# Four chained layers on one core: blocks for the mixed matrices made by ScalarE and GpSimd from rows loaded twice, and the mask multiplied on the returning mixed matrix

## The reference, cut to what matters

```python
x = x + L0(x, cond_8)   # top 2 of 8 experts per batch + one shared expert: (gelu(x Wg) * (x Wu)) Wd, inner width 1024
x = x + L1(x, cond_8)   # w_bot = einsum('bg,got->bot', y, weight * mask[None]); x @ w_bot^T + bias
x = x + L2(x, cond_8)   # x W_base^T + b_base + 2 * lora, ranks weighted by cond_8
x = x + L3(x, cond_8)   # one of 8 experts per batch: (silu(x Wu + bu) * (x Wg + bg)) Wd + bd, inner width 512
```

## Time and profile before

| | us |
|---|---|
| median of three runs | 1377.16 |
| lowest and highest | 1370.75, 1379.93 |
| the profiled execution | 1381.71 |
| its span, first to last instruction | 1380.1 |
| PE busy | 1278.1 (93%) |
| DVE busy | 707.0 (51%) |
| POOL busy | 619.6 (45%) |
| ACT busy | 414.5 (30%) |
| share of span that DMA queues' packets took | 16.6% SyncE's, 14.7% GpSimd's |

### The profile page before, as it was taken

The page is one execution under the profiler, slowest core; times in us unless marked ns, Lnnn a source line. Parts: engine busy times, 40 slices in busy tenths (PEclk is TensorE's granted clock), DMA queues, the critical chain, the costliest instruction groups (busy, mean ns, idle before and its releaser), DMA issues.

```text
span 1380.1 us, 29485 instructions
## 1 busy us (share of the span) xinstructions
PE 1278.1 (93%) x8230; PEld 1160.4 (84%) x8231; DVE 707.0 (51%) x1163; ACT 414.5 (30%) x816; POOL 619.6 (45%) x409
## 2 busy tenths in 40 slices
PE   8776897999999999999999999899999985999997
PEld 7676887888888888888888889899898974888886
DVE  6944453544545445454544544767777752333333
ACT  4122332232222222222222222334233321333332
POOL 4900046703425053442544800876656648888000
PEclk9988898999999999999999999999999997999999
DMA  7359993301213022121312210222322213444111
GB/s 199 100 128 263 253 264 90 106 14 44 76 30 89 13 61 61 42 76 30 91 42 76 61 61 15 70 92 92 108 84 83 78 49 99 133 128 132 44 44 39
DMA packets 134578, 122.82 MB, mean 89 GB/s; under 512 B 66033, under 2 KB 116465, under 8 KB 134529
## 3 DMA queue, kind: packets, MB, share of 16 engines
q1 hardware_dynamic: 116880, 59.71, 16.6%
q0 software_dynamic: 17648, 62.48, 14.7%
HBM read 88.07 MB, written 25.69 MB: 82 GB/s over the span
## 4 chain that ended last, share of the span: by engine, by line
PE 70%; POOL 10%; SPq 7%; DVE 5%; issue 5%; DMA 2%; ACT 1%; POOLq 0%; DVEq 0%; ACTq 0%
PE bank L590 12%; PE bank L591 12%; PE bank L592 12%; PE bank L642 5%; PE bank L644 5%; PE bank L643 5%; SPq L285 5%; POOL Wl L395 5%; PE bank L627 4%; POOL Wh L393 4%; PE bank L942 1%; PE bank L686 1%; PE bank L941 1%; PE bank L940 1%; PE bank L687 1%
## 5 line engine op out<-in xcount | busy, mean ns | idle before, releaser
L393 POOL TENSOR_TENSOR Wh<-raw,one 128x1024 fp32r<-128x1024 f32 x111 | 214.6, 1934 | 431.2 <-PE bank L644 286.5
L1434 DVE TENSOR_TENSOR FS<-bank,FS 128x512 f32<-128x512 f32 x200 | 138.0, 690 | 283.6 <-PE bank L592 241.2
L395 POOL TENSOR_TENSOR Wl<-raw,Wh 128x1024 fp32r<-128x1024 f32 x111 | 274.8, 2476 | 8.7
L590 PE MATMUL bank<-Wh,RS 128*128 (+1 forms) x576 | 226.3, 393 | 2.9 <-DVE Wl L1524 2.5
L1021 ACT ACTIVATE FS<-bank 128x512 f32<-128x512 f32 x200 | 119.7, 598 | 355.3 <-PE bank L592 354.8
L591 PE MATMUL bank<-Wl,RS 128*128 (+1 forms) x576 | 225.8, 392 | 0.0
L592 PE MATMUL bank<-Wh,RS 128*128 (+1 forms) x576 | 224.4, 390 | 0.0
L642 PE MATMUL bank<-Wh,RS 128*128 (+1 forms) x576 | 175.3, 304 | 4.9 <-DVE RS L1438 4.9
L644 PE MATMUL bank<-Wh,RS 128*128 (+1 forms) x576 | 163.3, 283 | 0.0
L643 PE MATMUL bank<-Wl,RS 128*128 (+1 forms) x576 | 163.1, 283 | 0.0
L590 PE MATMUL bank<-RS,Wh 128*128 128x256 f32 x448 | 136.2, 304 | 6.1 <-issue 6.1
(11 more groups left out here) (213 smaller groups left out, 2570.0 us busy)
## 6 DMA issues: line engine op xcount, KB each, us to landing
raw<-in_w POOLq DMA_DIRECT2D x83, 512.0 KB, 4.1
mixes<-acc SPq DMA_DIRECT2D x16, 1024.0 KB, 6.0
raw<-mixes POOLq DMA_DIRECT2D x32, 512.0 KB, 4.7
FS<-in_xT SPq DMA_DIRECT2D x200, 64.0 KB, 2.2
FS<-x SPq DMA_DIRECT2D x72, 64.0 KB, 2.1
out_rows<-FS SPq DMA_DIRECT2D x72, 64.0 KB, 2.0
acc<-in_x SPq DMA_DIRECT2D x32, 128.0 KB, 3.4
x<-raw SPq DMA_DIRECT2D x16, 256.0 KB, 2.2
```

The lines of the kernel that those rows point to most:

```text
L393: pool.tensor_tensor(hi, raw[:, k, :], ones_like(PIECE), ALU.mult).then_inc(done, 1)
L395: pool.tensor_tensor(lo, raw[:, k, :], hi.bitcast(F32), ALU.subtract).then_inc(done, 1)
L590: pe.matmul(ps, ah, bh, start=(i == 0), stop=False)
L1434: TT(hid[h], up_ps[h][:, :], gl[h], ALU.mult).then_inc(hid_done, 1)
```

## The change

- The stack of block n is made in place. GpSimd's queue loads eight pieces w1 (512 KB each), in which every 32 rows of the weight stand twice, unmasked. ScalarE copies 64 partitions to the stack as the high half (`stack`, 64x1024), GpSimd subtracts on the other 64 for the low half. Blocks 0 to 3 are made in the pair before the mixing stage, block n + 4 after step 2n + 1. The 64 DMAs in SBUF, the 32 mask DMAs and GpSimd's twelve operations on masked pieces are gone, and expert 0's splits wait for the last low half alone.
- The mask comes as two 128x256 tiles, one behind the last store, one into a spare slot of `acc` after the last expert sum. GpSimd multiplies each half of the returning matrix by it (128x1024, the mask broadcast over four batches), ScalarE makes the high half (`mixed_hi`), GpSimd the low half. Before, GpSimd made high and low half.
- ScalarE's and VectorE's order in a late unit is written anew.

```diff
-            def stack(n):
-                sp.wait_ge(w_step, 3 * (n // 4) + 3)
-                if n >= 4:
-                    for k in range(2):
-                        sp.wait_ge(mixed_in[k], 2 * (n - 4) + 2)
-                rows_ = slice(32 * (n % 4), 32 * (n % 4) + 32)
-                for q, src in enumerate((w_hi, w_hi, w_lo, w_lo)):
-                    sp.dma_start(stacked[n % 4][32 * q:32 * q + 32, :].bitcast(F32), src[n // 4][rows_, :].bitcast(F32))\
-                        .then_inc(stack_in[n % 4], 16)
...
             sp.wait_ge(tables_ready, 1)
+            sp.dma_start(mask1[:, :], mask[1]).then_inc(mask_in, 16)
...
+            load_late(0)
+            load_late(1)
+            sp.wait_ge(acc_done, S1)
+            sp.dma_start(maskt[0], mask[0]).then_inc(mask_in, 16)
+            load_late(2)
...
+            for n in range(WPIECES):
+                k = n // 2 % NRAW
+                if n % 2 == 0:
+                    pool.wait_ge(raw_in[k], 16 * (n // 6) + 16)
+                pool.wait_ge(stack_hi, n + 1)
+                here, there = half_rows(n), half_rows(n + 1)
+                at = stacked[n % 4]
+                pool.tensor_tensor(at[there, :], raw[here, k, :], at[here, :].bitcast(F32), ALU.subtract)\
+                    .then_inc(stack_lo, 1)
+                pool.wait_ge(stack_lo, n + 1)
+                if n % 2 == 1 and n // 2 + NRAW < WPIECES // 2:
+                    load(k, w1[n // 2 + NRAW])
...
             def mix_in(n, buffer, after=None):
-                for c in range(DC):
+                for i, c in enumerate((1, 0)):
                     pool.wait_ge(raw_in[c], at_raw[c] + 16 * n + 16)
-                    split(c, MAT + 2 * PIECE * buffer + PIECE * c, mix_split, 4 * n + 2 * c)
-                if after is not None:
-                    load_mix(after)
+                    here = raw[:, c, :].rearrange("p (q b r) -> p q b r", q=8, b=4)
+                    by_batch = maskt[c].rearrange("p (q r) -> p q r", q=8).unsqueeze(2).broadcast_to([P, 8, 4, 32])
+                    pool.tensor_tensor(here, here, by_batch, ALU.mult).then_inc(masked, 1)
+                for i, c in enumerate((1, 0)):
+                    at = MAT + 2 * PIECE * buffer + PIECE * c
+                    pool.wait_ge(mix_hi, 2 * n + i + 1)
+                    pool.tensor_tensor(Wl[:, at:at + PIECE], raw[:, c, :], Wh[:, at:at + PIECE].bitcast(F32),
+                                       ALU.subtract).then_inc(mix_split, 1)
+                    pool.wait_ge(mix_split, 2 * n + i + 1)
+                    if after is not None:
+                        src = mixes[bass.ds(after, 1), :, c * PIECE:(c + 1) * PIECE].rearrange("a p n -> p (a n)")
+                        load(c, src)
...
+            pool.wait_ge(mask_in, 32)
             mix_in(0, 0, after=1)
...
+            def stack(n):
+                k, here = n // 2 % NRAW, half_rows(n)
+                if n % 2 == 0:
+                    act.wait_ge(raw_in[k], 16 * (n // 6) + 16)
+                if n >= 4:
+                    act.wait_ge(mixed_in[1], 2 * (n - 4) + 2)
+                act.activation(stacked[n % 4][here, :], raw[here, k, :], ACT.Copy).then_inc(stack_hi, 1)
...
             gelu_late(0, 2)
+            mixed_hi(0, 0)
             hidden_hi_late(0, 1)
...
                 hidden_hi_late(k, 1)
+                mixed_hi(n + 1, 0)
                 x2_hi(n)
...
-                x2_hi(n + 1)
                 hidden_hi_late(k, 3)
+                mixed_hi(n + 2, 1)
+                x2_hi(n + 1)
...
                 x2_lo(n)
-                hidden_lo_late(k, 1)
                 join(n + 1, UE - 1 + k, late=k - 1)
-                hidden_late(k, 2)
                 if not last:
                     split_unit(k + 1, 1 - xset)
+                hidden_lo_late(k, 1)
+                hidden_late(k, 2)
```

More of the change, by code:

```diff
@@ L184, in build @@
         cond_rows_in, y_step, y_ready = sem("cond_rows_in"), sem("y_step"), sem("y_ready")
-        w_step = sem("w_step")
-        stack_in = [sem(f"stack_in{k}") for k in range(4)]
+        stack_hi, stack_lo = sem("stack_hi"), sem("stack_lo")
+        masked, mix_hi = sem("masked"), sem("mix_hi")
         mixed_in = [sem(f"mixed_in{k}") for k in range(2)]
@@ L322, in store_x3 @@
                              x3out.rearrange("p (t d) -> p t d", t=2)).then_inc(x3_stored, 16)
-            for t in range(3):
-                load_late(t)
+            load_late(0)
[3 more added lines that the diff above has]
+            load_late(2)
             store_x3(0, 0)
@@ L396, in split @@
                 pool.wait_ge(done, first + 2)
-            def load_mask(n):
-                for e in range(E):
-                    pool.dma_start(raw[e::E, 1, :], mask[n]).then_inc(mask_in, 16)
             pool.wait_ge(first_in[5], 16)
-            load(0, w1[0])
-            load_mask(0)
-            load(2, w1[1])
+            for m in range(NRAW):
+                load(m, w1[m])
             pool.wait_ge(diag_ready, 1)
@@ L469, in _ @@
                 load(i, w0_piece(first_chosen, i))
-            for k in range(4):
-                pool.wait_ge(stack_in[k], 16 * WPIECES)
             expert(0, 1, first_chosen, expert_at(chosen0, 1, E), stacks=True)
@@ L1048, in mix @@
                         mix_out(mixes_from + i)
+                        if i % 2 == 1 and (mixes_from + i) // 2 + 4 < WPIECES:
+                            stack((mixes_from + i) // 2 + 4)
+                    elif first and i % 2 == 1:
+                        stack(i // 2)
                 gelu(0, 2 * g)
@@ L1693, in unit @@
                 x2_lo(n + 1)
+                if not last:
+                    join(n + 2, k + 1)
                 hidden_lo_late(k, 3)
                 if not last:
-                    join(n + 2, k + 1)
                     hidden_late(k + 1, 0)
```

47 lines of the change are left out of this document (20 added, 27 removed).

## The result

The changed kernel took 1400.48 us (median of 4 runs, 1397.02 to 1402.94) against 1375.77 us in the runs of the kernel before beside it: ratio 1.0187, 95% interval 1.0147 to 1.0226, so 1.9% slower. Forecast were 1392 us. The profiled execution took 1402.1 us (span 1400.5) against 1381.71 before.

What follows compares the result with a forecast made beforehand. TensorE, busy 500.00 of 500.00 us from 300 to 800 us, was taken as the bound, with only its waits around that movable. Terms -9.2 + 2.7 - 1.5 + 5.8 + 16.8 = +14.6 on 1377.2 gave 1392 us; 8-in-10 range 1360 to 1409.

Steps and rivals of the forecast that it cites:

- Part 2: Mixing stage: fewer block DMAs save 6.5 us, but later first stores cost 9.2; sum +2.7 us (-5 to +8).
- part 3: Into the expert stage: VectorE's low half is no longer held, -2.1 us, mask DMA issue +0.6; sum -1.5 us.
- Part 5: Late-stage units: ScalarE's two copies push x2 by 2.1 us; fourteen halves, 7 x (1.3 + 1.1) = +16.8 us (0 to 29).
- Part 4: Start of the late stage: GpSimd waits for the second mask half, then its chain delays TensorE; +5.8 us (3 to 8).
- Part 1: Before the mixing stage: TensorE's waits of 4.51 and 4.91 us go, clock rises, table block held; -9.2 us (-12 to -5).
- Rival B: Mixing stage: first stores of the four pairs no longer make TensorE wait; -28 us there, total 1361 us; chance 0.12.
- Rival A: Late units: ScalarE's copies are absorbed, VectorE regains time lost to GpSimd, so 0 there; total 1375 us; chance 0.28.
- Rival C: Late units: GpSimd becomes the bound and ScalarE waits for its products, one us per half; 1406 us; chance 0.07.

Runs made afterwards that it cites:

- x4: The change with two of each pair's four stores of mixed pieces put ahead of the x loads on SyncE's queue: 1381.5 us, 1.0046 of before.
- x9: The kernel before with two of each pair's four stores, and the block transfers behind them, ahead of the x loads: 1375.3 us, ratio 0.9947.
- x11: The change with both mask products made from the early-loaded mask tile, the other tile, its load and wait left out: 1402.8 us, 1.0183 of before.
- x6: The change with GpSimd's four operations of each mixed matrix cut from 1024 to 128 columns: 1369.4 us, 0.9917 of before.
- x7: The change with ScalarE's two copies of each mixed matrix cut from 1024 to 128 columns: 1378.0 us, 0.9995 of before.
- x3: The change with ScalarE's two copies of the mixed matrix put ahead of its hidden high half: 1391.7 us, 1.0112 of before.
- x5: The change's front with half the stores ahead of x loads, late stage of before, mask multiplied on raw weight rows: 1354.0 us, 0.9820 of before.

## Why the prediction was right in its sign and short in its size

In the profiles the kernel lost 20.4 us where the sum has 14.6, and in the medians 24.7. That the total comes as near as this is in part luck: parts 2, 3 and 5 came out 10.9 us worse than the sum, and part 4, the expert stage, the last stage and part 1 5.0 us better.

**Part 1** (-9.2): right, -9.4. The waits of 4.51 and 4.91 us are gone. The copy of 64x2 that took 2.89 us takes 0.16, and the first operation of the table block is held by the last low half, 2.79 us:

```profile
38.87 0.16 DVE L1333 COPY routing<-routing 64x2 f32<-64x2 f32 x1
...
65.90 2.79 DVE L1392 TENSOR_TENSOR routing<-routing 64x476 f32<-64x476 f32 x1
```

The granted clock from 65 to 70 us was 0.80 against 0.66.

**Part 2** (+2.7) and **part 3** (-1.5): to the resumption at 214.38 they made +3.5, against +1.2. The mechanism was the one named: the first pair's wait is 7.27 us, forecast 7.1. Missing from the sum were VectorE's own late evictions, 4.0 us in three waits, the first at 115.86 (2.52 us) behind its routing block, one of whose operations is now held by GpSimd:

```profile
110.02 2.53 DVE L1426 TENSOR_SCALAR routing<-routing 1x104 f32<-1x104 int32 x2
```

Before, the same two took 0.33 us. In the expert stage another 0.9 us came off, where 0 was forecast. Rival B was well argued as to the place and wrong as to the means: a shorter queue alone left the waits, and x4 shows that most of them go with another order of it. x9 shows that the order alone, in the long queue, does not do it either. The page "DMA: Bandwidth & Descriptors" of the Trainium skill, section "Queues, rings and completion order", has each DMA engine take turns between the queues, by which the w1 loads would lengthen the stores. The median store took 6.6 us from issue to landing after and 6.0 before, which agrees; no run here has these loads as its only difference.

**Part 4** (+5.8): +4.1. The term that was too large is the chain of GpSimd: I had ScalarE's second copy follow both products and both low halves follow it, 11.7 us. The first copy ran beside the second product, and the chain took 10.3, from 861.95 to 872.26. x11 shows the rest: even the wait for the mask is worth nothing in the end.

**Part 5** (+16.8, from 0 to 29): right in its mechanism and too small in its size. The late stretch grew by 25.4 us, and the fourteen halves that the sum counts by 27.9 (241.2 to 269.1); a unit grew by 4.0 us (33.7 to 37.7), where 2.4 were forecast. The copies sat where I put them, between the hidden copy and x2, and moved x2 by the 2 us that I had. What was mis-sized is the half with the smaller slack: I had the choice between 1.1 us ("the floor, since the join in front of it holds the port") and 2.55 us, if GpSimd's low half catches the hidden low. It does, and holds it for 3.02 us at 997.72, and the join in front is not held at all. TensorE waits 1.00 us for x2 and then 1.2 us more at the ranks (1.18 in the half shown), and this half lasts 18.1 us instead of 16.0: 2.1 us more, not 1.1. With the upper value the same sum gives 7 x (1.3 + 2.55) = 27 us. x6 and x7 show the two terms separately, 3.1 and 3.3 us a unit over the undisturbed 30.8. Of the 4.0 us more a unit, the copies make 3.1, the holds 0.4 (3.3 in place of the 2.9 that before paid), and the rest comes with both together. The sum also took every half of before as one with holds, while four of its early ones, at 15.4 to 16.2 us, paid next to nothing.

**Rival A** (the copies are absorbed and VectorE gets its time back) is out as a forecast of the time: x3 is its best case, with the copies in the idle time, and still lies 16 us above before in the late stretch. The rule of the Trainium skill that bears on it ("SBUF — State Buffer", section "Who interferes with whom") is that a VectorE operation with two inputs in SBUF contends with GpSimd, and one with at most one such input only in the modes that use two ports. VectorE's operation with one input in PSUM and one in SBUF ran inside GpSimd's product of 985.97 to 988.75 at its usual length:

```profile
987.38 0.69 DVE L1452 TENSOR_TENSOR FS<-bank,FS 128x512 f32<-128x512 f32 x1 [0.89 <-ACT FS L1017]
```

That agrees with the rule. The copy of 64x2 that took 2.89 us has one input in SBUF and was held; no run shows in which mode it ran. Half of the rival came true: VectorE's holds fell from 50.8 to 34.8 us in the late stretch, although GpSimd still made four operations per matrix. The error was to take that for time of TensorE's. ScalarE's copies were not absorbed, and the holds that stayed stand in the chain that TensorE waits for.

**Rival C** (GpSimd is the bound) did not happen: its product with the broadcast mask took 2.40 us, one of the two now and then 2.78 (at 985.97, when VectorE had started 0.16 us ahead of it), and ScalarE never waited long for it.

## What to carry to other kernels

An instruction that moves to an engine with much idle time costs its full length if it is put behind the wait and not ahead of it: look on which side of the releasing event it stands. Then look at which operations of the engine that is held up stand in the chain that TensorE waits for: here VectorE got 16 us back and TensorE waited no less for it. And before shortening a queue, read what its head waits for: moving two stores ahead of loads was worth 19 us in the change, and nothing in the mixing stage of the kernel before, where block transfers stood in the same queue.

## What was not expected of the hardware

Which of two operations is held cannot be read from their recorded starts. The hidden low half at 997.72 started 0.05 us before GpSimd's operation and took 3.02 us; a join in x3 started 0.27 us ahead (1010.35) and took 3.23. But the same form as the first, 0.16 us ahead of GpSimd's 985.97, took its usual time, and GpSimd's took 2.78 us instead of 2.40:

```profile
985.81 0.68 DVE L1460 TENSOR_TENSOR RS<-FS,RS 128x512 fp32r<-128x512 f32 x1
```

Where VectorE's 128x512 operation is the one that is held, it ends some 0.56 us behind GpSimd's: so the two at 997.72 and 1010.35, and the one at 216.73 before, beside GpSimd's from 217.06 to 218.96. Two x splits in a row can each be held, 4.95 us together in x5.

And one late stage with the same instructions took 274.1 to 283.9 us in five kernels that differ only ahead of it, while the stage with more copies took 309.3 to 310.6 in four. Up to the last quadruple the five take 253.5 to 258.0 us, the four 287.8 to 290.1. The rest of the spread is in the end behind it, where the clock differs. Why the halves ahead of it differ with the start is open: that a chain which meets GpSimd's operations at some phases keeps its phase for some units is a guess that no run here tests.
